# Projection tiles mixed within a step: three units of K, Q or V and one gate, begun a step earlier, in a macaron block with gated-delta attention

## The reference

```python
q = silu(conv4(x @ Wq, qcw, qcb))      # causal, 4 taps, per column
k = silu(conv4(x @ Wk, kcw, kcb)) * D ** (-0.5)
v = silu(conv4(x @ Wv, vcw, vcb))      # 16 heads of D = 128
alpha = sigmoid(x @ Wa + ba); beta = sigmoid(x @ Wb + bb)
for each token:                        # S is 128 x 128 for each head
    err = S @ k - v
    S   = alpha * S - beta * outer(err, k)
    o   = S @ q
o = layernorm(o) * ln_w + ln_b
out = (o * sigmoid(x @ Wg)) @ Wo       # back to 256 columns
feed-forward: down(silu(x @ gate_w) * (x @ up_w)), weights rounded to fp8, with scales
```

## Time and profile before

| | |
|---|---|
| time, median of 3 runs | 2321.36 us (2321.36 to 2321.77) |
| profiled execution | 2322.96 us, span 2321.2 us |
| mean granted clock of TensorE | 0.993 |
| busy: PE, ACT, POOL, DVE | 2231.4, 2048.9, 2021.2, 1987.5 us |
| steps that PE takes from its loop | 113 (s = 7 to 119), 28 periods of four |

### The profile page before, as it was taken

One profiled execution on the slowest core, in us unless ns is written; L12 is line 12 of the kernel. 1 busy time (PEld: TensorE's weight loads), 2 busy tenths in 40 slices (PEclk: granted clock), 3 DMA queues, 4 the chain that ended last, 5 costly groups with the idle time before them and its releaser, 6 DMA issues.

```text
span 2321.2 us, 66819 instructions
## 1 busy us (share of the span) xinstructions
PE 2231.4 (96%) x25520; PEld 1660.5 (72%) x25520; DVE 1987.5 (86%) x4283; ACT 2048.9 (88%) x4148; POOL 2021.2 (87%) x2159
## 2 busy tenths in 40 slices
PE   5999999999999899999998999999989999999999
PEld 2555677777777677777776777777767777777765
DVE  8889888889888788888888998888888888888644
ACT  3886899999999899999998999999989999988765
POOL 4875799999999899999998999999988999989775
PEclk9999999999999999999999999999999999999999
DMA  5442222222222122222222222122321232222001
GB/s 139 129 145 70 45 47 48 47 45 42 45 72 56 47 48 47 48 47 48 62 62 50 47 46 42 46 48 47 84 53 38 48 68 44 42 47 47 13 28 46
DMA packets 174236, 128.93 MB, mean 56 GB/s; under 512 B 122848, under 2 KB 135136, under 8 KB 173792
## 3 DMA queue, kind: packets, MB, share of 16 engines
q1 hardware_dynamic: 173920, 124.66, 23.7%
HBM read 85.69 MB, written 13.77 MB: 43 GB/s over the span
## 4 chain that ended last, share of the span: by engine, by line
PE 73%; DVE 5%; POOL 4%; ACT 3%; issue 1%; DMA 1%; SPq 0%; ACTq 0%; POOLq 0%; DVEq 0%
PE bank L3276 23%; PE bank L3247 7%; PE bank L3100 4%; PE bank L3140 3%; PE bank L3210 3%; PE bank L3345 3%; PE bank L3114 3%; PE bank L3211 3%; DVE k_rows L1751 3%; PE bank L3112 3%; PE bank L3224 2%; PE bank L3038 2%; PE bank L3040 2%; PE bank L3039 2%; PE bank L3383 2%; PE bank L3130 2%
## 5 line engine op out<-in xcount | busy, mean ns | idle before, releaser
L1751 DVE SCALAR_TENSOR_TENSOR k_rows<-bank,k_prm,k_rows 128x509 f32<-128x509 f32 (+2 forms) x1152 | 842.4, 739 | 9.1 <-ACT k_rows L2361 4.5
L3276 PE MATMUL bank<-k_z,k_kqv 128*128 128x512 f16 x2304 | 644.8, 379 | 18.9 <-DVE k_rows L1751 18.6
L2470 ACT ACTIVATE k_wide<-bank 128x512 f16<-128x512 f32 x640 | 374.2, 596 | 44.5 <-PE bank L3114 41.1
L1683 DVE TENSOR_TENSOR k_y<-bank,k_masks 128x256 f16<-128x256 f32 x768 | 316.0, 415 | 70.4 <-PE bank L3100 69.6
L2361 ACT ACTIVATE k_rows<-bank,k_prm 128x512 f32<-128x512 f32 x384 | 297.9, 776 | 28.2 <-PE bank L3276 26.6
L3100 PEld LDWEIGHTS bank<-k_wide 128*128 128x128 f16 x3072 | 154.7, 97 | 152.6 <-ACT k_wide L2470 72.9
L3114 PE MATMUL bank<-k_wide,k_y 128*128 128x64 f16 x3072 | 257.3, 193 | 0.8 <-DVE k_y L1683 0.8
L3112 PE MATMUL bank<-k_y,k_wide 128*128 128x64 f16 x2560 | 236.5, 193 | 5.3 <-DVE k_y L1683 4.9
L1251 POOL TENSOR_TENSOR k_wide<-k_solve,k_ident 128x512 f16<-128x512 f32 x128 | 163.9, 1280 | 83.3 <-DVE k_solve L1662 80.8
L3276 PEld LDWEIGHTS bank<-k_z,k_kqv 128*128 128x128 f16 x2304 | 176.4, 98 | 79.0 <-DVE k_rows L1751 21.9
L3112 PEld LDWEIGHTS bank<-k_y,k_wide 128*128 128x128 f16 x2560 | 192.0, 98 | 57.1 <-DVE k_y L1683 40.2
(11 more groups left out here) (176 smaller groups left out, 6861.3 us busy)
## 6 DMA issues: line engine op xcount, KB each, us to landing
a_decay<-decay_rows SPq DMA_DIRECT2D x128, 258.0 KB, 4.4
k_solve<-cumulative_rows SPq DMA_DIRECT2D x96, 258.0 KB, 3.9
weight_pairs<-k_wide SPq DMA_DIRECT2D x15, 512.0 KB, 2.9
k_kqv<-weight_pairs SPq DMA_DIRECT2D x9, 512.0 KB, 4.1
stream<-in_L_attn_x SPq DMA_DIRECT2D x8, 512.0 KB, 7.8
out<-stream SPq DMA_DIRECT2D x7, 512.0 KB, 2.9
k_rows<-in_L_attn_Wk SPq DMA_DIRECT2D x4, 512.0 KB, 4.6
k_rows<-in_L_attn_Wq SPq DMA_DIRECT2D x4, 512.0 KB, 5.2
```

The lines of the kernel that those rows point to most:

```text
L1683: nc.vector.tensor_tensor(even(y16[:, j], mb), bank[LEV[par]][:, 0:U * C // 2].rearrange("p (u b m) -> p u b m", u=U, m=mb), masks[:, j].r ...
L1751: nc.vector.scalar_tensor_tensor(out=dst[:, d:S], in0=bank[PJ[j % 2]][:, 0:S - d], scalar=prm[:, i, U * (n // B) + j, TAPS - 1 - d:TAPS - ...
L2470: nc.scalar.activation(both, bank[LEV[par]][:, :].rearrange("p (two b m) -> p two b m", two=2, m=mb), ACT.Copy).then_inc(m[f"act_lev{par}" ...
L3276: mm = pe.matmul(bank[PJ[j % 2]][:, :], wt, z16[:, zh, k, cols], start=(x == 0), stop=(x == 5))
```

## The change

Which tiles a step projects is put in a table, and "tile" is told apart from "slot": slot (v, h) is the place h of step v, and holds unit j of kind i. From the third sequence on, slots 0 to 2 of each step hold K, Q or V, and slot 3 a gate. The four gates of a sequence thus stand in the four steps, the last of them in the first step after. The projection's functions take a slot and look the tile up; banks go by slot, PJ[h % 2]; waits for a finished projection count by the tile's place.

All five lists are written anew for it. PE's step now holds `project(s + 1, ...)` beside `gram_k(s - 2)`, where it held `project(s + 2, ...)` beside `gram_k(s)`: a tile is begun a step earlier against the chunk's own work. POOL's loop starts at a lower chunk, so its prologue is shorter. SP's list changes in one thing: the loads of the K, Q, V and gate weights stand one step earlier, that of Wo where it stood. POOL gets two waits on DMAs that are complete by then. The number of instructions of each function stays.

```diff
-WO_PLACE = KINDS + 2
+WO_PLACE = KINDS + 3
+MIXED_FROM = 2
+TILES = (((0, 0), (0, 1), (0, 2), (3, 3)), ((0, 3), (1, 0), (1, 1), (3, 0)),
+         ((1, 2), (1, 3), (2, 0), (3, 1)), ((2, 1), (2, 2), (2, 3), (3, 2)))
...
+    def tile(v, h):
+        n, r = divmod(v, NC)
+        if n < MIXED_FROM:
+            return v, h
+        i, j = TILES[r][h]
+        return NC * (n - (r == 0 and h == U - 1)) + i, j
...
+    def slot_before(v, h):
+        x = U * v + h - 2
+        while x >= 0 and not placed(*divmod(x, U)):
+            x -= 2
+        return divmod(x, U)
...
         def load_pairs(s):
-            group, place = divmod(s - NC * (B - 1) + 2, NC * B)
+            group, place = divmod(s - NC * (B - 1) + 3, NC * B)
...
-        def project(t, j, part):
+        def project(v, h, part):
...
-                before, other = (t, j - 2) if j >= 2 else (t - 1, j + 2)
-                if known(before):
-                    pe.wait_ge(*tile_done(before, other))
+                before, other = slot_before(v, h)
+                if before >= 0:
+                    pe.wait_ge(*tile_done(*tile(before, other)))
...
-                mm = pe.matmul(bank[PJ[j % 2]][:, :], wt, z16[:, zh, k, cols], start=(x == 0), stop=(x == 5))
+                mm = pe.matmul(bank[PJ[h % 2]][:, :], wt, z16[:, zh, k, cols], start=(x == 0), stop=(x == 5))
...
         def step(s):
+            first_solution(s - 4)
+            project(s, 3, 2)
...
```

More of the change, by code:

```diff
@@ L1479, in _ @@
[L1479 to L1495, removed]
         for s in range(5, STEPS - 8):
             step(s)
+        first_inverse(STEPS - 13)
+        query_low(STEPS - 13)
+        w_low(STEPS - 15)
@@ new lines, in _ @@
+        scaled_k(STEPS - 14)
+        low(STEPS - 16)
+        root(STEPS - 15)
+        key_low(STEPS - 12)
+        system_low(STEPS - 13)
+        strengths(STEPS - 11)
+        scaled_q(STEPS - 14)
+        state(STEPS - 14)
+        system16(STEPS - 12)
+        first_inverse(STEPS - 12)
+        query_low(STEPS - 12)
+        gated(STEPS - 15)
+        w_low(STEPS - 14)
+        scaled_k(STEPS - 13)
+        low(STEPS - 15)
+        root(STEPS - 14)
+        strengths(STEPS - 10)
+        scaled_q(STEPS - 13)
@@ new lines, in _ @@
+        level(STEPS - 6, 5)
+        level(STEPS - 5, 1)
+        mixing(STEPS - 5)
+        output(STEPS - 8)
+        decays(STEPS - 4)
+        level(STEPS - 5, 2)
+        system(STEPS - 4)
+        residual(STEPS - 6)
+        tap(STEPS - 1, 0, 1)
+        corrected(STEPS - 6)
+        level(STEPS - 5, 3)
+        tap(STEPS - 1, 1, 1)
+        tap(STEPS - 1, 0, 2)
+        tap(STEPS - 1, 1, 2)
+        tap(STEPS - 1, 0, 3)
+        statistics(STEPS - 6)
+        level(STEPS - 4, 0)
+        aggregated(STEPS - 6)
@@ L2775, in _ @@
         gate(7, 2)
-        normed(3)
+        one(7, 2)
         for s in range(6, STEPS - 8):
             step(s)
-        silu(STEPS - 7, 1)
+        affine(STEPS - 12)
+        first_solution(STEPS - 11)
+        query_high(STEPS - 9)
+        level(STEPS - 10, 2)
+        high(STEPS - 12)
+        level(STEPS - 10, 3)
+        w_decayed(STEPS - 11)
+        w_high(STEPS - 11)
+        first_inverse(STEPS - 9)
+        level(STEPS - 9, 0)
+        level(STEPS - 10, 4)
+        level(STEPS - 9, 1)
@@ L2790, in _ @@
-        acc(STEPS - 6, 1)
-        w_decayed(STEPS - 10)
-        w_high(STEPS - 10)
-        first_inverse(STEPS - 8)
-        query_high(STEPS - 8)
-        level(STEPS - 9, 3)
         high(STEPS - 11)
         acc(STEPS - 6, 2)
+        silu(STEPS - 6, 1)
+        gate(STEPS - 6, 3)
+        query_high(STEPS - 8)
+        one(STEPS - 7, 3)
+        w_decayed(STEPS - 10)
+        first_inverse(STEPS - 8)
+        level(STEPS - 9, 3)
+        acc(STEPS - 5, 0)
+        key_high(STEPS - 7)
+        w_high(STEPS - 10)
@@ L2856, in _ @@
-        one(STEPS - 5, 3)
+        silu(STEPS - 3, 1)
+        level(STEPS - 7, 5)
+        gate(STEPS - 3, 3)
+        first_solution(STEPS - 7)
+        level(STEPS - 6, 1)
+        silu(STEPS - 3, 2)
+        affine(STEPS - 8)
+        acc(STEPS - 2, 0)
+        silu(STEPS - 3, 0)
+        level(STEPS - 6, 2)
+        acc(STEPS - 2, 1)
+        w_decayed(STEPS - 7)
+        w_high(STEPS - 7)
         query_high(STEPS - 5)
-        acc(STEPS - 3, 0)
-        level(STEPS - 6, 2)
-        w_decayed(STEPS - 7)
@@ new lines, in _ @@
+        read(STEPS - 12, 0, U // 2)
+        read(STEPS - 12, U // 2, U)
+        project(STEPS - 7, 1, 2)
+        level_a(STEPS - 11, 4)
+        first_inverse(STEPS - 10)
+        v_turned(STEPS - 11)
+        gram_q(STEPS - 10)
+        level_a(STEPS - 10, 0)
+        update(STEPS - 12)
+        level_b(STEPS - 11, 4)
+        level_b(STEPS - 10, 0)
+        output(STEPS - 13)
+        project(STEPS - 7, 2, 0)
+        project(STEPS - 7, 2, 1)
+        level_a(STEPS - 11, 5)
+        project(STEPS - 7, 2, 2)
```

1863 lines of the change are left out of this document (927 added, 936 removed).

## The result

The changed kernel takes 2411.26 us (median of 4 runs, 2409.13 to 2413.92) where the kernel before takes 2321.57: a ratio of 1.0387, with a 95% interval of 1.0375 to 1.0400. It is slower by 90 us; forecast were 8 us less.

A forecast was written before the change was run, and what follows sets the result against it. PE was taken as the bound, 59.64 of 60.20 us a period. Steady steps -1.4 us, Wo's load -7, start and end 0: against the median 2321.36 - 8.4 = 2313 us, own range 2304 to 2320, overall 2288 to 2336.

The forecast's parts named there:

- the second rival: Steady steps, chunks 0 to 2: POOL sets the pace at 15.5 us a step; +21 us, about 2342 us; chance 0.18.
- POOL's lag: Steady steps: put at 0.1 us a period, within the 1.0 us of PE waits expected after the change.
- The taps' waits: PE's projections waiting for a tap, 18.6 us in 33 waits: expected to go, -0.56 us a period.
- 13.6 forecast: DVE's load with nine taps in every steady step: about 13.6 us a step.
- the copies that I named: ACT's copies that PE waits for: first inverse, 0.5 us at chunk 0; a level, 0.4 us at chunk 3.
- Wo's waits: `output` waiting for Wo's load in three steps: 5.44 us becomes about 4.1; with the clock's part, -7 us in all.
- The steady steps' own gain: Steady periods: waits of 1.0 us after against 1.05 before, -0.05 x 28 = -1.4 us.
- PE's own 59.1 us: PE's own work in a four-step period: 60.20 - 0.56 - 0.5 us, expected to stay.
- The start and the end: First and last steps, with both lists re-laid: taken as 0, with 5 us to either side.

The follow-up runs named there:

- the scan held back: Changed kernel, with DVE's scan of the decays also waiting until POOL has issued the first two operations of `root`: 2344.07 us, ratio 1.0090 to the kernel before.
- both repairs: Changed kernel, with the scan waiting behind the root's first two operations up to the last step and Wo's load at the head of SP's step: 2328.98 us, ratio 1.0020.
- the root first: Changed kernel, with POOL's `root` exchanged to stand ahead of `key_low`: 2385.96 us, ratio 1.0280.
- the kernel before with the earlier scan: Kernel before, with DVE's scan of the decays ahead of `new_state`, 0.66 us earlier: 2367.83 us, ratio 1.0199.

## Why the prediction was wrong

**The step that failed** stands under the second rival: "POOL's work isn't touched by mixing (56.49 us a period ...)", with the price of 15.5 us a step, and "POOL's lag I put at 0.1" in the sum. POOL's instructions are the same, their durations are not: they depend on what DVE does beside them, and the change re-lays DVE's list. The direction of that rival, POOL setting the pace at chunks 0 to 2, came true; its price, +1.0 us a period, was +2.8 because the fullest steps take 16.0 to 16.1 us and not 15.5, and a held operation of the root stands on the chain in the fourth step too. I took durations from one order as constants of another.

The clue stood in the profile before. Of the root's four operations on 4 columns, two took 203 to 206 ns and `a_shift`, of the same shape, 523 ns in the mean. The prediction asks of no operation what runs beside it. The one operation in DVE's loop that has both inputs in SBUF is the scan, and the new list puts it two entries behind `aggregated`, the operation that releases the root.

**Steps that held.** The taps' waits went (33 to 4), with DVE at 13.4 to 14.0 us a step against 13.6 forecast. With the scan out of the way, ACT's waits come at the copies that I named, a level's and the first inverse's. What PE waited for in the five periods of the run with the scan held back, all rows:

```profile
PE bank L3170 <- ACT k_wide L2519: 1.2, 5, 0.2
PE bank L3170 <- ACT k_wide L2536: 1.0, 5, 0.2
```

That is one of each a period, 0.24 us for the first inverse and 0.20 for the level, about half of the 0.5 and 0.4 forecast. Wo's waits fell to 12.2 us in 3, 4.07 each against "about 4.1", and the gain of 7 to 9 us answers to the 7 forecast.

**The steady steps' own gain** did not come. Forecast were 59.1 + 1.0 = 60.1 us a period, 0.05 less than before; with the scan out of the way it is 60.47, 0.35 more. PE's waits in it are 0.44 us, less than the 1.0 forecast, so the term that is not borne out is PE's own 59.1 us, which rests on an estimate of 0.5 us of waits hidden in stretched rows. What fills the difference stays open.

**The start and the end**, taken as 0 with 5 us to either side, cost about 10 us each in the changed kernel, and the scan's wait repairs little of it. With it, the first inverse of chunk 8 is at 351.73, still 7.2 us later than before, and from that of chunk 112 (1941.67) to the end of the span (2342.2) it takes 10.2 us more than before. The start scatters from one execution to the next: with both repairs, where the lists up to there are those of the scan's wait alone, it is at 356.29. Part of the start is work done ahead: by the first inverse of chunk 8, PE has issued 270 projection matmuls where it had issued 252, three units, or 18 x 0.216 = 3.9 us at PE's usual spacing. Most of the end's loss lies between the first inverses of chunks 116 and 120, where the loop ends; after, then before:

```profile
2069.50:2137.50 68.00, 61.26 (x735) 47.36 (x734) 54.72 (x117) 55.89 (x115) 56.56 (x60) 1.00 0.18 39
1991.10:2050.50 59.40, 58.26 (x725) 44.24 (x721) 53.27 (x119) 55.80 (x117) 54.72 (x59) 1.00 0.24 46
```

PE is idle 6.7 us there where it was idle 1.1. Which order of which engine makes it so is not shown.

## What to carry to other kernels

When a list is re-laid, take each operation of VectorE with both inputs in SBUF, look what GpSimd will start beside it, and add the hold to GpSimd's load before you call it unchanged. Equal operations with unequal means in the old profile were the sign here that such a hold exists, even where it costs nothing yet. Where a collision can't be avoided by order, make the long operation wait until the other engine is past the operations that it would hold: here one semaphore wait was worth 67 us. Before you take an exchange of two neighbours as a test of a hold, see whether one of the two is on the path itself. And ask of each DMA that an engine waits for what stands ahead of it in its queue: moving one load past one wait gave more than the whole re-layout was forecast to give.

## What was not expected of the hardware

A power on four columns (1.01 us) that starts 0.10 us or more ahead of the scan isn't held, and does not hold the scan: in the kernel before and with the wait, scan and power run side by side at 1.23 and 1.01 us. But a start just ahead of the scan does not save it. With the root first, in the fourth step, the power starts 0.04 us ahead, takes 2.06 us and ends 0.8 us after the scan:

```profile
999.28 2.06 POOL L1361 TENSOR_TENSOR a_rstd<-a_var,k_nhalf 128x4 f32<-128x4 f32 x1
```

```profile
999.32 1.23 DVE L1694 TENSOR_TENSOR_SCAN a_prod<-a_decay,k_diag 128x516 f32<-128x516 f32 x1
```

The `a_nmean` of 438.52 above, 0.02 us ahead, was likewise held, by 1.04 us for 0.2 us of work. The hold goes the other way as well. In the kernel before with the earlier scan, the scan of 957.35 starts while this operation of POOL is under way, and takes 1.46 us instead of 1.22:

```profile
956.53 1.19 POOL L1288 TENSOR_TENSOR k_narrow<-k_rows,k_solve 128x512 f32<-128x512 f32 x1
```
